# First stage's gate network folded into mean weights, second chunk's variance on ScalarE, and the projections' transposes ahead of the attended values

## What is computed

```python
x = x + ln(dilated_attention(ln(x)))              # softmax(q k^T / sqrt(128)) v in segments of 64, dilation 4, q = k = v
x = x + ln(ternary_linear(hadamard_quantised(ln(x))))   # 4 bit activations, ternary weights
n = ln(x)
q_mean = mean over 16 heads of (n @ w_q.T)        # 64 features for each token
H = (q_mean - mean) * rsqrt(var + eps) * ln_g + ln_b
scores = gelu(H @ w1.T + b1) @ w2.T + b2          # w1 is 16 x 64; top 32 tokens of each batch are kept
x = x + ln(attention whose dots are scaled by sigmoid(kept scores))   # 16 heads of 64
h = x + gqa(rmsnorm(ln(x)))                       # 16 heads, 4 kv heads, causal
x = x + ln(h + moe(rmsnorm(h)))                   # top 2 of 8 experts
```

## Time and profile before

| | us |
|---|---|
| median of 3 runs | 642.27 |
| lowest, highest | 640.20, 647.02 |
| profiled execution, device time | 641.33 |
| its span, first to last instruction | 639.6 |

### The profile page before, as it was taken

How to read it: one execution, slowest core, us unless ns; L and a number is a source line. 1 busy time by engine, 2 the same in 40 slices (tenths; PEclk the granted TensorE clock), 3 DMA queues, 4 the chain that set the end, 5 groups by cost and what they waited for, 6 DMA issues and landing times. The chain is left out here.

```text
span 639.6 us, 11630 instructions
## 1 busy us (share of the span) xinstructions
PE 536.4 (84%) x3754; PEld 299.9 (47%) x3754; DVE 485.3 (76%) x2125; ACT 369.1 (58%) x829; POOL 248.8 (39%) x474
## 2 busy tenths in 40 slices
PE   1876577977989997679999999999998898999971
PEld 0876567975676563112333333333333455456420
DVE  6499878367665667889799999999997156369786
ACT  4962255610534564014687788878788665466864
POOL 2001044744001333102445454544555454266764
PEclk9987665557997998555899999999999989899996
DMA  8000000110000694200111111111110000000001
GB/s 325 9 1 2 0 34 35 66 26 8 1 2 9 169 250 130 62 3 5 32 39 37 34 38 35 55 45 39 32 40 2 7 2 1 1 2 17 17 34 66
DMA packets 18875, 27.32 MB, mean 43 GB/s; under 512 B 3230, under 2 KB 14126, under 8 KB 18638
## 3 DMA queue, kind: packets, MB, share of 16 engines
q1 hardware_dynamic: 18174, 24.34, 12.9%
q10 hardware_dynamic: 576, 2.10, 0.9%
q0 software_dynamic: 64, 0.13, 0.1%
HBM read 14.11 MB, written 12.45 MB: 42 GB/s over the span
## 5 line engine op out<-in xcount | busy, mean ns | idle before, releaser
L982 DVE CUSTOM_DVE_ANT_0 w_qkvT<-d_pS,w_qkvT 128x512 bf16<-128x512 f32 x480 | 203.9, 486 | 16.8 <-PE d_pS L973 11.7
L1651 ACT ACTIVATE d_P<-pT 128x768 f32<-128x768 f32 (+1 forms) x192 | 165.9, 882 | 62.7 <-PE pT L1677 61.0
L1531 POOL TENSOR_SCALAR_AFFINE_SELECT d_P<-d_P 128x256 f32<-128x256 f32 x256 | 103.1, 417 | 133.6 <-ACT d_P L1651 133.6
L973 PE MATMUL d_pS<-Ks,Qs 48*128 48x512 bf16 x480 | 97.9, 325 | 12.8 <-DVE hadamard L982 8.9
L1677 PE MATMUL d_pO<-d_P,V 128*32 128x512 f32 (+3 forms) x1024 | 98.5, 460 | 1.4 <-POOL d_P L1531 0.9
L1677 PE MATMUL pT<-Qs,Ks 51*128 51x512 bf16 (+3 forms) x512 | 72.8, 312 | 2.0 <-ACT d_mT L1621 2.0
L973 PEld LDWEIGHTS d_pS<-Ks,Qs 48*128 48x128 bf16 x480 | 32.3, 96 | 56.1 <-DVE hadamard L982 51.9
L1677 PEld LDWEIGHTS pT<-Qs,Ks 51*128 51x128 bf16 x512 | 20.7, 94 | 74.1 <-ACT d_P L1651 42.7
L982 DVE DVE_READ_ACCUMULATOR2_ANT hadamard<- 128x1 f32 x512 | 42.7, 83 | 0.0
L1994 ACT ACTIVATE e_T<-pT,comb 128x128 f32<-128x128 f32 x88 | 25.1, 381 | 22.7 <-issue 15.0
L1677 PEld LDWEIGHTS d_pO<-d_P,V 128*32 128x32 f32 x1024 | 21.2, 110 | 32.3 <-issue 29.5
(11 more groups left out here) (336 smaller groups left out, 1051.7 us busy)
## 6 DMA issues: line engine op xcount, KB each, us to landing
Qs<-q_stack SPq DMA_DIRECT2D x32, 192.0 KB, 3.2
...
```

Of the source, the lines that this page charges most:

```text
L973: last = nc.tensor.matmul(dst[:, at:at + w], top.Qs[c][rows, h % 8, 128 * q:128 * q + 128], top.Ks[c][rows, h // 4 % 2, 0:w], start=True, ...
L982: last = nc.vector.tensor_tensor_reduce(out=junk[:, at:at + w], in0=src[:, at:at + w], in1=top.wide_mask[:, 512 - w:512], scale=1.0, scala ...
L1531: last = nc.gpsimd.affine_select(out=view, in_=view, compare_op=ALU.is_ge, fill=0.0, base=0, pattern=[[0, 2], [1, 128]], channel_multiplie ...
L1651: nc.scalar.activation(P[pair % 4][:, :, P_AT[unit]:P_AT[unit] + w], pT[(3 * pair + unit) % 2][:, :, 0:w], ACT.Exp, scale=float(HD4) ** -0 ...
```

## The change

Three things change, and the written order around them.

1. **Gate network of stage 1.** The mean-q weights, the gain of the layer norm and `w1` become one matrix `fold` of 64 + 16 columns, made once by four small matmuls and a few DVE instructions (`mean_weights`, `weights_home`, `fold_home`, `folded_weights`). `means` now writes 80 columns: 64 centred features and the 16 inputs of the gate before their scale. The variance is a sum of squares on ACT (`squares3`, 8 instructions) and `qvariance` on DVE; `gate` is now three DVE instructions (reciprocal, times, plus `offset`). `qstats`, `qnorm`, ACT's `normalise3`, `turned_z`, `gained`, PE's `gate` and POOL's four `ones_row` memsets go.
2. **Round 1 and the rows of round 3.** `normalise1` of chunks 1 and 3 moves from ACT to DVE; chunk 1's variance is by `squares1(1)` and `variance1(1)` in place of `ostats1(1)`; `normalise3(3)` moves from POOL to DVE. The orders of all queues of stage 1 are written anew.
3. **Projection phase.** ACT does `normalise(turn)` behind `deviations_x(turn)` in the same turn, where it did `normalise(turn - 1)` first in the turn. PE does `by_channel(turn-1)` ahead of `attended(turn+1)`, and the second `keep_busy` of 4 stands only in turns without an `attended`.

```diff
 def weights_home():
     dve.wait_ge(sm["parts_psum"], 1)
-    dve.wait_ge(sm["centred_psum"], 1)
+    dve.wait_ge(sm["gain_psum"], 1)
+    nc.vector.tensor_copy(w_meanT[:, :], turned_mean)
+    nc.vector.tensor_copy(spread[:, DH:DH + PROJ], gain_psum).then_inc(sm["turned"], 1)
+    nc.vector.tensor_copy(offset[:, :], offset_psum).then_inc(sm["offset_row"], 1)
...
-    nc.vector.tensor_copy(top.w_qmeanT[:, :], centred).then_inc(sm["centred"], 1)
+def fold_home():
+    dve.wait_ge(sm["fold_psum"], 1)
+    nc.vector.tensor_copy(fold[:, :], fold_psum).then_inc(sm["fold"], 1)
...
+def normalise1(c):
+    for t in range(CT):
+        last = nc.vector.tensor_scalar(n[c][:, t, :], X[c][:, t, :], mv["s1_"][c][:, t, 0:1],
+                                       rs1[c][:, t:t + 1], ALU.subtract, ALU.mult)
...
-def qstats(c):
-    dve.wait_ge(sm["s3_qm"], done[c])
-    moments(lambda t: PS[c][:, t, 0:DH], c, "s3_q")
+def qvariance(c):
+    dve.wait_ge(sm["s3_qss"], done[c])
+    dve.wait_ge(sm["s3_small"], done[c])
+    nc.vector.scalar_tensor_tensor(out=qvar[c][:, :], in0=ss[c][:, :], scalar=1.0 / DH, ...)
-def qnorm(c):
+def gate(c):
     dve.wait_ge(sm["s3_qstd"], done[c])
     nc.vector.reciprocal(qrs[c][:, :], qstd[c][:, :]).then_inc(sm["s3_qrstd"], 1)
...
+    nc.vector.tensor_tensor(pre[c], PS[c][:, :, DH:DH + PROJ], <qrs broadcast>, ALU.mult)
+    nc.vector.tensor_tensor(pre[c], pre[c], <offset broadcast>, ALU.add).then_inc(sm["s3_pre"], 1)
...
-def normalise3(c):      # ACT: 8 activations into z
-def gained(c):          # ACT
+def squares3(c):
+    act.wait_ge(sm["s3_qm"], done[c])
+    for t in range(CT):
+        last = nc.scalar.activation(nT[c][:, t, 0:DH], PS[c][:, t, 0:DH], ACT.Square,
+                                    accum_out=ss[c][:, t:t + 1])
...
-        last = mm(PS[c][:, t, 0:DH], nT[c][:, t, :], top.w_qmeanT[:, :])
+        last = mm(PS[c][:, t, 0:DH + PROJ], nT[c][:, t, :], fold[:, :])
-def turned_z(c):        # PE: 8 transposes
-def gate(c):            # PE: 8 products by w1T
...
 for turn in TURNS:      # ACT, projection phase
-    if turn - 1 in batches:
-        normalise(turn - 1)
     if turn - 2 in batches:
         second_part(turn - 2)
     if turn - 1 in batches:
         by_channel(turn - 1)
     if turn in batches:
         deviations_x(turn)
+        normalise(turn)
...
 for turn in TURNS:      # PE, projection phase
-    if turn + 1 in batches:
-        attended(turn + 1)
     if turn - 1 in batches[:LAST]:
         keep_busy(turn - 1, 4 if turn > 1 else 12)
         by_channel(turn - 1)
-        keep_busy(turn - 1, 4)
+    if turn + 1 in batches:
+        attended(turn + 1)
+    else:
+        keep_busy(LAST - 1, 4)
+    if turn - 1 in batches[:LAST]:
         project(turn - 1)
```

More of the change, by code:

```diff
@@ L99, in dilated_and_ternary_phase @@
             small(name) for name in ("std2", "top2", "sc", "rsc", "sq2", "small2", "var2", "ostd2", "ors2", "ss"))
-        std3, rs3, small3, qvar, qstd, qrs, qnb = (
-            small(name) for name in ("std3", "rs3", "small3", "qvar", "qstd", "qrs", "qnb"))
+        std3, rs3, small3, qvar, qstd, qrs = (
+            small(name) for name in ("std3", "rs3", "small3", "qvar", "qstd", "qrs"))
         w = ph.sb("w", [128, D])
@@ L111, in dilated_and_ternary_phase @@
         ternT = PS[0][:, 4, :]
-        centred = PS[0][:, 6, 0:DH]
+        turned_mean = PS[0][0:DH, 5, :]
+        gain_psum = PS[0][0:DH, 6, 0:PROJ]
+        offset_psum = PS[0][:, 7, 0:PROJ]
+        fold_psum = PS[0][:, 4, 0:DH + PROJ]
+        w_meanT = ph.sb("w_meanT", [DH, D])
+        gains = ph.sb("gains", [DH, PROJ])
+        spread = ph.sb("spread", [DH, DH + PROJ])
+        biases = ph.sb("biases", [DH + 1, D])
+        fold = ph.sb("fold", [128, DH + PROJ])
+        offset = ph.sb("offset", [128, PROJ])
         done = [c + 1 for c in chunks]
@@ L330, in score @@
                         .then_inc(sm["s3_score"], 1)
-                stats1(0); stats1(1); norm1(0); stats1(2); norm1(1); stats1(3)
-                norm1(2); ternary_weights(); norm1(3); mean_weights(); sums(0); sums(1)
-                ostats1(0); ostats1(1); add1(0); add1(1); stats2(0); stats2(1)
+                stats1(0); stats1(1); norm1(0); stats1(2); norm1(1); normalise1(1); norm1(2)
+                stats1(3); ternary_weights(); norm1(3); normalise1(3); mean_weights(); sums(0); ostats1(0)
+                sums(1); variance1(1); add1(0); add1(1); stats2(0); stats2(1)
                 sums(2); sums(3); variance1(2); quantise(0); variance1(3); add1(2)
-                weights_home(); add1(3); clamp(0); quantise(1); stats2(2); variance2(0)
-                quantise(2); add2(0); stats2(3); stats3(0); quantise(3); qstats(0)
-                clamp(1); qnorm(0); clamp(2); clamp(3); norm3(0); variance2(1); add2(1)
-                variance2(2); stats3(1); add2(2); norm3(1); variance2(3); stats3(2)
-                add2(3); qstats(1); qnorm(1); stats3(3); norm3(2)
-                qstats(2); norm3(3); qnorm(2); qstats(3); qnorm(3)
+                weights_home(); add1(3); fold_home(); clamp(0); quantise(1); stats2(2); clamp(1)
+                variance2(0); stats2(3); add2(0); quantise(2); variance2(1); add2(1)
+                quantise(3); clamp(2); stats3(0); clamp(3); stats3(1); norm3(0); norm3(1)
+                variance2(2); add2(2); variance2(3); add2(3); qvariance(0); stats3(2); stats3(3)
+                gate(0); qvariance(1); norm3(2); norm3(3); gate(1); normalise3(3)
+                qvariance(2); gate(2); qvariance(3); gate(3)
                 score(0); score(1); score(2); score(3)
@@ L468, in _ @@
                 nc.gpsimd.memset(top.ones_bf[:, :], 1.0).then_inc(sm["ones"], 1)
-                ones_row(0); ones_row(1); ones_row(2); ones_row(3); normalise3(0); normalise3(1)
-                normalise3(2); normalise3(3)
+                nc.gpsimd.memset(biases[:, :], 1.0).then_inc(sm["ones"], 1)
+                normalise3(0); normalise3(1); normalise3(2)
             @block.tensor
```

113 lines of the change are left out of this document (59 added, 54 removed), and 6 rows, old and new, of the table sm.

## The result

The changed kernel takes **620.5 us** in the median of 4 runs (619.9 to 621.2) against 642.3 of before: a ratio of 0.965, 95% interval 0.961 to 0.970. That is 21.7 us less where 15.6 were forecast. The profiled execution has a span of 618.2 us.

| us | before | after | change | forecast |
|---|---|---|---|---|
| stage 1 | 132.3 | 109.9 | -22.4 | -14.6 |
| gated attention | 55.1 | 58.4 | +3.3 | 0 |
| projections, to the last rest of the queries | 69.2 | 67.1 | -2.1 | -1.0 |
| all behind | 383.0 | 382.9 | -0.1 | 0 |

What follows compares the result with a forecast made beforehand. Stage 1 was taken as bound by DVE's queue plus a 12 us tail, the projections by PE; -14.6 us in stage 1 and -1.0 in the projections gave -15.6, a median of 626.6 us, 80% range 618.5 to 635.5.

Steps and rivals of the forecast that it cites:

- parts 2 and 3: Stage 1 behind the first add1: DVE's work 70.4 us, 73.4 with small gaps, plus waits of 4.5 in place of 19.3.
- The rival that the waits come back: Stage 1's last third: each of four chunks waits 3 us instead of 1, 8 us return, 634.6 us; chance 0.13.
- Part 4: Stage 1: DVE's normalise3(3) is held beside POOL's normalise3(2), 0.5 us for each of eight instructions, costing 4 us.
- No blocking: Stage 1: normalise3(3) on DVE slips between POOL's instructions at no cost; 622.6 us, 621 with a warm start; chance 0.15.
- Part 1: Stage 1 up to the first add1: it starts at 34.1 us, a gain of 1.7 us.
- warm case: Start of stage 1: PE warms after three groups, attended(1) ends at 29.5 and add1(0) starts at 33.1.
- cold one: Start of stage 1: PE stays slow to the fifth group and add1(0) starts at 35.0.
- The other three phases only shift: Phases other than stage 1 and the projections hold none of the changed code and only move in time.
- Part 5: Projections: turns of 7.2 us but an earlier first rest of the queries; -1 us, bounds -3 and +6.
- The ring: Projections: DVE and ACT wait on each other in a cycle through normalise's new place, 7.2 us a turn.
- What follows is as before: Projections: after the rest of batch 6 starts, at 244.0 where it was 245.27, nothing further changes.
- The clock rival: Projections: turns stay at PE's half clock; all six 653 us, chance 0.05; two to three about 635, chance 0.07.

Runs made afterwards that it cites:

- experiment 5: Changed kernel with the fourth chunk's normalise3 back on GpSimd, so GpSimd does all four: 623.3 us.
- experiment 8: Changed kernel with two unused two-operand additions on GpSimd ahead of its normalise3(2): 622.3 us.
- experiment 11: Changed kernel with GpSimd's fills of the key and value tiles made to wait until VectorE has taken the gathered rows: 616.8 us, ratio to before 0.960.
- experiment 12: Changed kernel with GpSimd's key and value fills later and the projections' ScalarE and TensorE orders of the kernel before: 616.0 us, ratio to before 0.958.
- experiment 1: Changed kernel with the projections' ScalarE and TensorE orders put back, leaving the stage 1 change alone: 619.6 us, ratio to before 0.967.
- experiment 9: Changed kernel with TensorE's order alone put back in the projections (attended values first, then transposes): 623.4 us.
- experiment 4: Changed kernel with 14 keep-warm matmuls in the gated attention, filling TensorE's gap before VectorE's copy of the queries: 618.9 us.

## Why the prediction was right, and where it was off

- **The mechanism of stage 1** (parts 2 and 3) came as worked out: DVE's idle time behind the first `add1` is 76.48 - 69.39 = 7.1 us, forecast 4.5 + 3; the squares of the second round, 6.9 us before, are no longer waited for, those of the gate for 0.8 us (forecast 1.3), and nothing stands on PE behind `means(3)`. Its work is 69.4 us against 70.4. The rival that the waits come back is out. (The five waits of before add up to 19.5 us, not 19.3; nothing hangs on it.) No run takes the folded gate network out by itself: that it ended these waits is read from the traces of before and after.
- **Part 4 is the term that was mis-sized**: taken at +4 us, measured 0. Experiments 5, 8 and 11 show why: GpSimd's TENSOR_SCALAR does not hold VectorE, its additions and fills do, and the work itself lay in a wait. The first rival, *No blocking*, is what happened, and its 621 us with a warm start is the measured time. That it fits so well is luck: without the 3.3 us lost in the gated attention it would have been some 617 us (620.5 - 3.3, an estimate), below the range of 618.5 to 635.5.
- **Part 1**: 3.8 us instead of 1.7. I had `sums(0)` at 24.9 and it came at 24.86; behind it `add1(0)` came 1.1 us ahead of my warm case and 3 ahead of my cold one, since PE's products had their short durations after two groups of eight tiles, where the warm case had three: `attended(1)` ended at 28.3, not 29.5.
- The sum 34.1 + 73.4 + 4.5 + 4 = 116.0 stands against 32.0 + 69.4 + 7.1 = 108.5: 4.0 from part 4, 2.1 from part 1, 1.4 from work and waits.
- **"The other three phases only shift"** was wrong for the gated attention: +3.3 us, without a changed instruction. PE's clock fell behind an idle gap of 3 us in it, and with the gap at 0.5 us (experiments 11 and 12) it did not. How much is lost varies without an edit: experiments 1 and 9 start the phase at the same 109.9 with the same instructions, and it took 56.8 and 56.6 us. I had put this risk on the projections alone.
- **Part 5**: turns of 7.04 us (forecast 7.2), and -2.1 us for the phase (forecast -1, bounds -3 and +6). The ring is as described. That the phase came out shorter is not the ring's merit but a short slow stretch's: alone it was worth 0.1 us. "What follows is as before" did not hold either: the last turn grew from 11.3 to 12.3 us, with `normed` held and a longer slow stretch. The clock rival there did not come true in the changed kernel; experiment 9 shows a price for it, two turns longer by 0.7 us each and a first rest 2.6 us later.

Not settled: what makes the slow stretches fall where they fall. In every trace there is one within the first 10 us of the projections. No run here tried to move it, and the net effect of lifting the clock in one place (experiment 4) was half of what the place itself gained.
